# A convolution, attention and mixture-of-experts kernel: wider products, one part of each weight split moved, 24 places for gathered rows

## The reference, cut to what matters

```python
# x: (16, 16, 16, 192) float32, i.e. 4096 tokens of 192 channels
xs = gelu(x @ W1.T + b1)                 # 192 -> 48 channels
xs = abs(low_pass(xs))                   # fft2, mask, ifft2 over each 16x16 image
x  = x + (xs @ W2.T + b2)                # 48 -> 192
t  = x.reshape(16, 256, 192)
n  = layernorm(t)
q, k, v = n@Wq+bq, n@Wk+bk, n@Wv+bv      # 12 heads of 16; one k and one v head
t  = t + softmax_over_heads(rope(q).rope(k) / 4) @ v   # each token attends inside itself
n  = layernorm(t)
p  = softmax(n @ gate_w.T)               # 8 experts, the best 2 with weights p1/(p1+p2), p2/(p1+p2)
y  = sum over the 2 of  weight * ((silu(n @ gate_bank[e]) * (n @ up_bank[e])) @ down_bank[e])
out = t + y
```

## Time and profile before

| | |
|---|---|
| profiled execution | 475.46 us, span of the trace 473.7 us |
| convolution phase | 0 to 74 us |
| attention phase | 74 to 185.3 us |
| routing phase | 185.3 to 222 us |
| expert phase | 222 to 473.7 us |
| mean granted TensorE clock | 0.88 of 2.4 GHz |
| busy: PE, DVE, ACT, POOL | 394.8, 276.5, 222.0, 280.7 us |

### The profile page before, as it was taken

One profiled execution on the slowest core, in us unless ns is written; L12 is line 12 of the kernel. 1 busy time (PEld: TensorE's weight loads), 2 busy tenths in 40 slices (PEclk: granted clock), 3 DMA queues, 4 the chain that ended last, 5 costly groups with the idle time before them and its releaser, 6 DMA issues.

```text
span 473.7 us, 9033 instructions
## 1 busy us (share of the span) xinstructions
PE 394.8 (83%) x2236; PEld 373.5 (79%) x2237; DVE 276.5 (58%) x718; ACT 222.0 (47%) x513; POOL 280.7 (59%) x302
## 2 busy tenths in 40 slices
PE   5799954779888585176789999999999999999990
PEld 5799943668777474065689999999999999999990
DVE  1265683387667622997156666666666666666650
ACT  3434420434555441085245555555565556555550
POOL 0256561277777642001637877887878788787753
PEclk9999999976888555555689999999999999999996
DMA  7998532003333534200314444444445444444442
GB/s 213 245 230 227 145 68 63 25 1 103 104 102 116 148 99 137 24 0 12 104 21 68 75 78 68 72 79 72 72 73 79 68 72 77 70 73 74 59 44 25
DMA packets 46087, 41.27 MB, mean 87 GB/s; under 512 B 14153, under 2 KB 40108, under 8 KB 46060
## 3 DMA queue, kind: packets, MB, share of 16 engines
q0 software_dynamic: 14016, 17.21, 22.8%
q1 hardware_dynamic: 32044, 23.75, 18.9%
HBM read 25.87 MB, written 15.08 MB: 86 GB/s over the span
## 4 chain that ended last, share of the span: by engine, by line
PE 48%; DMA 2%; issue 1%; another core or an unknown queue 1%; ACT 0%; POOLq 0%; DVE 0%; SPq 0%; ACTq 0%; DVEq 0%
PE moe_ps_y L1137 8%; PE moe_ps_h L1123 5%; PE moe_ps_gt L1112 3%; PE moe_ps_gt L1116 3%; PE moe_ps_gt L1113 3%; PE moe_ps_gt L1115 3%; PE moe_ps_gt L1114 3%; PE moe_ps_u L1112 3%; PE moe_ps_y L1139 3%; PE moe_ps_u L1113 3%; PE moe_ps_u L1114 3%; PE moe_ps_u L1115 3%; PE moe_ps_u L1116 3%; PE moe_ps_x L1104 2%; PE moe_ps_x L1103 2%; PE moe_ps_y L1136 2%
## 5 line engine op out<-in xcount | busy, mean ns | idle before, releaser
L1078 POOL DMA_INDIRECT out<-moe_y,idx_map x72 | 114.6, 1592 | 39.8 <-issue 20.2
L1070 POOL DMA_INDIRECT moe_xt<-rows,idx_map x72 | 70.5, 979 | 55.7 <-POOLq L865 34.0
L1213 ACT ACTIVATE moe_yy<-moe_ps_y,moe_xt 128x384 f32<-128x384 f32 x72 | 41.9, 583 | 71.9 <-PE moe_ps_y L1137 58.0
L1137 PE MATMUL moe_ps_y<-wd,moe_h_hi 128*128 x216 | 71.6, 356 | 0.7 <-DVE moe_h_lo L1275 0.5
L1283 DVE TENSOR_TENSOR moe_y<-moe_yy 128x192 f32<-128x192 f32 x72 | 25.8, 359 | 57.1 <-ACT moe_yy L1213 47.7
L1193 ACT ACTIVATE moe_x_hi<-moe_ps_x 128x256 fp32r<-128x256 f32 x72 | 27.7, 385 | 38.2 <-PE moe_ps_x L1104 32.1
L1275 DVE TENSOR_TENSOR moe_h_lo<-moe_ps_h,moe_h_hi 128x384 fp32r<-128x384 f32 x72 | 40.2, 559 | 5.7 <-ACT moe_h_hi L1205 3.6
L1137 PEld LDWEIGHTS moe_ps_y<-wd,moe_h_hi 128*128 128x128 f32 x216 | 41.3, 191 | 1.3 <-issue 1.3
L1269 DVE TENSOR_TENSOR moe_hid<-moe_ps_u,moe_sg 128x384 f32<-128x384 f32 x72 | 39.4, 548 | 1.2 <-issue 1.2
L1259 DVE TENSOR_TENSOR moe_x_lo<-moe_ps_x,moe_x_hi 128x128 fp32r<-128x128 f32 x72 | 21.0, 292 | 31.8 <-ACT moe_x_hi L1193 25.3
L1205 ACT ACTIVATE moe_h_hi<-moe_ps_h 128x384 fp32r<-128x384 f32 x72 | 35.5, 493 | 4.0 <-remote 2.4
(11 more groups left out here) (188 smaller groups left out, 1124.2 us busy)
## 6 DMA issues: line engine op xcount, KB each, us to landing
xs<-in_x SPq DMA_DIRECT2D x8, 384.0 KB, 5.1
conv_stage<-in_wgu SPq DMA_DIRECT2D x8, 384.0 KB, 3.8
conv_stage<-in_wgu SPq DMA_DIRECT2D x16, 192.0 KB, 4.6
rows<-attn_xr SPq DMA_DIRECT2D x8, 384.0 KB, 2.7
out<-xs SPq DMA_DIRECT2D x8, 384.0 KB, 3.4
attn_stage<-in_down SPq DMA_DIRECT2D x8, 288.0 KB, 3.4
conv_xta<-in_xT SPq DMA_DIRECT2D x8, 256.0 KB, 4.3
moe_xt<-rows,idx_map POOLq DMA_INDIRECT x72
```

What stands on the lines that cost most here:

```text
L1070: nc.gpsimd.indirect_dma_start(xt[:, slot, :], None, rows.ap(), bass.IndirectOffsetOnAxis(ap=idx_map[:, j, 0:1], axis=0)).then_inc(gathere ...
L1078: nc.gpsimd.indirect_dma_start(out, bass.IndirectOffsetOnAxis(ap=idx_map[:, j, 1:2], axis=0), y[:, j % YR, :], None, compute_op=ALU.add).t ...
L1137: ins = nc.tensor.matmul(both, hi, halves, start=(k == 0), stop=(k == 2))
L1213: nc.scalar.activation(yy[:, s].rearrange("p h c -> p (h c)"), ps_y[:, s, 0:2 * C], ACT.Copy, scale=xt[:, slot, bass.ds(GC + e, 1)]).then_ ...
```

## The change

`XR` becomes 24, `AHEAD` 22, `YR` stays 12. `xs`, the norms' constants and the attention weights now give their room back after the attention phase, and the gathered rows lie there. The expert phase stops after 71 tiles; its loops are written out for 24 tiles; TensorE starts it with 16 matmuls whose result nobody reads, then the first transposes, then 4 more, and ScalarE with one activation of one column of the function Silu.

In the convolution phase `w1a` and `w1b` are padded with zeros to 128 columns, so that lines 240 and 241 make 128 columns; SP waits for these two memsets before its first load. `out_product` takes high and low parts stacked on 128 rows (`yt_hl`), so two matmuls do the work of three; `magnitude` has three activations for two, and the low part two subtractions for one. At the end of the phase SP issues the loads of all eight experts' down weights, straight into `wd`.

In the attention phase the router's rows are turned in six pieces of 128 columns for eight, and its logits come from three matmuls of 16 columns for each pair of tiles, six for eight. ScalarE makes all eight high parts of the down weights before `copy_products(0)`; POOL makes five of the low parts before `rotate_key(0)` and one more in each of the first three steps. POOL does `weigh_value(n)` before `deviation(n-1)`, ScalarE `exponential(n)` before `norm_route(n-2)`.

```diff
-XR = 12
+XR = 24
 AHEAD = XR - 2
-YR = XR
+YR = XR // 2
+TILES_USED = 2 * TOKENS // P + EXPERTS - 1
...
-        w1a, w1b = a.sb("w1a", [P, DH]), a.sb("w1b", [CB + 1, DH])
+        w1a, w1b = a.sb("w1a", [P, P]), a.sb("w1b", [CB + 1, P])
...
+                sp.wait_ge(wide, 2)
+                sp.dma_start(w1a[:, 0:DH], w1[0:P, :]).then_inc(w1_in, 16)
...
+                for e in range(EXPERTS):
+                    sp.dma_start(wd[:, e, :, 1, :].bitcast(F32),
+                                 down[e].rearrange("(k p) c -> p k c", p=P)).then_inc(down_in, 16)
...
-                            hi, lo = yt_hi[k, s, bass.ts(h, P)], yt_lo[k, s, bass.ts(h, P)]
-                            nc.tensor.matmul(at, hi, w2_hi[k, :], start=True, stop=False)
-                            nc.tensor.matmul(at, hi, w2_lo[k, :], start=False, stop=False)
-                            last = nc.tensor.matmul(at, lo, w2_hi[k, :], start=False, stop=True)
+                            both = yt_hl[:, s, m, bass.ts(h, P)]
+                            nc.tensor.matmul(at, both, w2_hi[:], start=True, stop=False)
+                            last = nc.tensor.matmul(at, both, w2_lo[:], start=False, stop=True)
...
-                    transposes(nc, xr[:, s], eye, ps_ra, ps_rb).then_inc(rtr_done, 1)
+                    for k in range(6):
+                        ...
+                        ins = nc.tensor.transpose(bank, flat[:, bass.ts(k, P)], eye[:])
...
-                        for t in range(QT):
-                            at = ps_q[:, s, 0, ps_lg.start + t * EXPERTS:ps_lg.start + (t + 1) * EXPERTS]
-                            nc.tensor.matmul(at, ra[:, bass.ts(t, P)], ga[:], start=True, stop=False)
-                            ins = nc.tensor.matmul(at, rb[:, bass.ts(t, P)], gb[:], start=False, stop=True)
+                        for h in range(2):
+                            pair = ps_q[:, s, 0, bass.ds(ps_lg.start + 2 * h * EXPERTS, 2 * EXPERTS)]
+                            for k in range(3):
+                                ins = nc.tensor.matmul(pair, ra[:, bass.ts(3 * h + k, P)], gates[:, bass.ts(k, 2 * EXPERTS)],
+                                                       start=(k == 0), stop=(k == 2))
...
                 out_of_psum(0, 0)
+                act.wait_ge(down_in, 16 * EXPERTS)
+                for e in range(EXPERTS):
+                    split(e)
...
                     if n < QUADS:
-                        split(*turned(0, n))
+                        exponential(*turned(0, n))
                     if 0 <= n - RING < QUADS:
                         norm_route(*turned(0, n - RING))
-                    if n < QUADS:
-                        exponential(*turned(0, n))
...
+                for e in range(EXPERTS - 3):
+                    split(e)
                 rotate_key(0, 0)
-                split(0, 0)
                 for n in range(QUADS):
                     if n + 1 < QUADS:
                         rotate_key(*turned(0, n + 1))
+                    weigh_value(*turned(0, n))
                     if n:
                         deviation(*turned(0, n - 1))
-                    weigh_value(*turned(0, n))
-                    if n + 1 < QUADS:
-                        split(*turned(0, n + 1))
+                    if n < 3:
+                        split(EXPERTS - 3 + n)
...
-                for j in range(N):
+                for j in range(TILES_USED):
                     scatter(j)
-                    if j + AHEAD < N:
+                    if j + AHEAD < TILES_USED:
                         gather(j + AHEAD)
...
+                def keep_busy(n):
+                    for _ in range(n):
+                        nc.tensor.matmul(ps_g[:, 0, 0:HID], wa_hi[:, 0, 0:P], wa_hi[:, 0, 0:HID], start=True, stop=True)
+                keep_busy(16)
                 turn_x(0, 0)
+                keep_busy(4)
```

More of the change, by code:

```diff
@@ L292, in _ @@
                 nc.scalar.activation(lp_hi[:], lp[:], ACT.Copy)
-                for k in (0, DP):
-                    b = slice(k, k + DH + 1)
-                    ins = nc.scalar.activation(w2_hi[b, :], w2s[b, :], ACT.Copy)
-                ins.then_inc(const_hi_done, 1)
+                nc.scalar.activation(w2_hi[:], w2s[:], ACT.Copy).then_inc(const_hi_done, 1)
                 def gelu(i, s):
@@ L313, in magnitude @@
                     act.wait_ge(yt_lo_done, freed(q))
-                    for dst in (yt, yt_hi):
-                        ins = nc.scalar.activation(dst[:, s, :], ps_f[:, s, 0:SEQ], ACT.Abs, bias=y_bias[:, 0:1])
+                    nc.scalar.activation(yt[:, s, :], ps_f[:, s, 0:SEQ], ACT.Abs, bias=y_bias[:, 0:1])
+                    for m in range(2):
+                        b = slice(DP * m, DP * (m + 1))
+                        ins = nc.scalar.activation(yt_hl[b, s, m, :], ps_f[b, s, 0:SEQ], ACT.Abs, bias=y_bias[b, 0:1])
                     ins.then_inc(abs_done, 1)
@@ L410, in yt_low @@
                     dve.wait_ge(w2_done, freed(q))
-                    nc.vector.tensor_tensor(yt_lo[:, s], yt[:, s], yt_hi[:, s].bitcast(F32),
-                                            ALU.subtract).then_inc(yt_lo_done, 1)
+                    for m in range(2):
+                        b, o = slice(DP * m, DP * (m + 1)), slice(DP * (1 - m), DP * (2 - m))
+                        ins = nc.vector.tensor_tensor(yt_hl[o, s, m, :], yt[b, s], yt_hl[b, s, m, :].bitcast(F32),
+                                                      ALU.subtract)
+                    ins.then_inc(yt_lo_done, 1)
                 def split(i, s):
@@ L500, in transposes, with attention_phase @@
     return ins
-def attention_phase(nc, xs, shift, rstd, eye, wqa, wqb, cos_t, sin_t, ga, gb, rows, row_tiles, down, wd, lg, out):
+def attention_phase(nc, xs, shift, rstd, eye, wqa, wqb, cos_t, sin_t, gates, rows, row_tiles, wd, down_in, lg, out):
     with ExitStack() as stack:
@@ L533, in attention_phase @@
         stored, filled, bias_row = a.sem("stored"), a.sem("filled"), a.sem("bias_row")
-        stage_in = [a.sem(f"stage_in{s}") for s in range(RING)]
         xn_done, tr_done, ev_done = a.sem("xn_done"), a.sem("tr_done"), a.sem("ev_done")
@@ L573, in store @@
                     sp.dma_start(out_tiles[:, bass.ts(q, QT), :], xs[:, bass.ts(q, QT), :]).then_inc(base_out[s], 16)
-                load_weights(0, 0)
-                load_weights(0, 1)
-                with sp.Fori(1, QUADS // RING) as i:
+                with sp.Fori(0, QUADS // RING) as i:
                     for s in range(RING):
-                        load_weights(i, s)
-                        store(i - 1, s)
-                for s in range(RING):
-                    store(last, s)
+                        store(i, s)
                 sp.wait_ge(stored, 16)
@@ L1149, in up_product, with steps @@
                     product(r, e, ps_u, HID, up_done)
-                def steps(i, first, last):
+                def steps(i, first, last, more=True):
                     e = {first: expert(i, first)}
@@ L1155, in steps @@
                         gate_product(i, r, e[r])
-                        if r + 1 < XR or last > XR:
+                        if more or r + 1 < last:
                             turn_x(i, r + 1)
@@ L1214, in weigh @@
                                          scale=xt[:, slot, bass.ds(GC + e, 1)]).then_inc(weighed, 1)
+                nc.scalar.activation(sg[:, 0, 0:1], eye[:, 0:1], ACT.Silu)
                 x_high(0, 0)
@@ L1233, in _ @@
                 n = N // XR - 1
-                for r in range(2, XR + 2):
-                    if r + 1 < XR:
+                for r in range(2, REST + 2):
+                    if r + 1 < REST:
                         x_high(n, r + 1)
-                    if r - 1 < XR:
+                    if r - 1 < REST:
                         h_high(n, r - 1)
-                    if r < XR:
+                    if r < REST:
                         silu(n, r)
@@ L1327, in _ @@
                 sp.wait_ge(meet_done, 1)
-                for j in range(1, N):
+                for j in range(1, TILES_USED):
                     if j > 1:
@@ L1332, in _ @@
                     sp.sem_inc(clear, 1)
-                for j in range(N - SR, N):
+                for j in range(TILES_USED - SR, TILES_USED):
                     landed(j)
```

115 lines of the change are left out of this document (58 added, 57 removed).

## The result

The changed kernel takes **481.56 us** (median of 4 runs, 479.83 to 483.24), the kernel before, beside it, 475.18 (470.65 to 477.8): ratio 1.014, interval 1.009 to 1.019. It is slower by 1.4%, clear of noise, and far above the 458.0 that was forecast. The profiled execution took 483.24 us with a span of 481.4, where before it was 473.7.

The account below looks back on a forecast made before the run. No single engine bounds all phases: TensorE the convolution, a three-engine ring attention, TensorE and POOL the experts. From 475.5 us, convolution -5.0, attention -9.4, routing 0 and experts -3.1 give 458.0; own range 452 to 464, of all 448 to 468.

Parts of the forecast that it names:

- What bounds the kernel, convolution: Convolution loop: TensorE bound at 7.05 us a quad, loads close behind at 6.4; the change gains 5.0 us.
- The start: Convolution: SP waits for two memsets before its first load, and loads bound the start; costs 0.8 us.
- `deviation` moves behind the weighting. The ring loses the deviation: Attention loop, POOL: the move takes the deviation out of the ring; periods fall from 10.5 to 9.1 us, 7.0 gained.
- the ring of the residual: Attention: product copy, key rotation, deviation, value weighting, residual, next copy over ScalarE, POOL and VectorE set the 10.60 us period.
- my 9.1: Attention: new period in us, taken between VectorE's 8.8 and TensorE's 9.2 with a low-clock spell.
- The first rival: Attention: TensorE at the low clock becomes the bound; half the periods so gives 466.4 us, all 475; chance 0.18.
- The collision of product and weighting: Attention: VectorE's product and POOL's weighting, side by side, take 2.29 and 1.95 us for 1.01 and 1.63.
- The tail: End of the attention phase: fewer router matmuls and transposes, less copy, 1.5 us given back by the deviation's move; 1.7 gained.
- the first scatter is at 250.4: Expert phase start: POOL issues 22 gathers at 1.25 us each, so the first scatter comes at 250.4, not 243.5.
- the second rival: Expert phase end: POOL's chain catches up at 4.8 us a scatter pair, TensorE's end counts, 8.7 gained for 3.1; chance 0.14.
- my 17.5 us: Whole kernel: the forecast gain, convolution 5.0, attention 9.4 and experts 3.1 us, from 475.5 to 458.0.
- the queue of gathers is too short: Expert phase, POOL: gathers 11 to 22 each wait for an older landing, first scatter 23 us late, 481 us; chance 0.06.

Follow-up runs that it names:

- the first four experiments: Changed kernel with 10 gathers ahead, 459.54 us; 12 places and 10 ahead, 457.01; 10 ahead then two behind each scatter, 466.14; no filling matmuls, 459.30.
- the fifth: The changed kernel run again unchanged, beside the kernel before: 461.50 us, ratio 0.979, first result 16.3 us after the first gather.

## Why the prediction was wrong

*What bounds the kernel, convolution.* Right. The in-products of quads 3 to 8 start 6.44 us apart in the mean ((50.03 - 17.84) / 5), in the 6.2 to 6.5 forecast, though single ones are 5.7 to 7.8 apart, at 239 GB/s. The clock did move, to 0.78 in the loop, up and down with each burst. The start came 0.6 us late, priced at 0.8. 4.0 us in this trace and 4.2 in the mean, for 5.0: in the tail a quad's out-products still wait 3.59 us, until 61.42, for VectorE's halves, so the faster clock gave less than 3.2.

*Attention.* Wrong in its step "`deviation` moves behind the weighting. The ring loses the deviation". The move added nothing that the traces show; the kernels with the split gone and the deviation left first are at least as short. The deviation left the ring of the residual and lengthened another that I had not drawn: copy and rotation (3.5 us), weighting (1.95), deviation (2.5), and on ScalarE the row norm (1.86), which stands ahead of the next copy in program order: with the gaps 9.9 us. I had asked what waits for POOL and forgotten that ScalarE's in-order stream carries the wait on to the copy, though the earlier trace rows and the kernel's text gave both the order and the durations. Seven periods gained 2.3 us (67.74 to 65.48) for 7.7: the last five take 50.8 us, where 9.1 each would be 45.5. The longer ring is a part of that and not the whole. With the deviation first four periods in three traces are down to 8.8 and 8.9, under my 9.1, but the five still take 50.3, 49.3 and 47.8 us. The first rival has another part: in twelve of the fourteen traces with the deviation behind, one or two of these periods are 10.5 to 11.3 us because the copy waits for TensorE, in this trace one, 11.25. What holds the other long periods no run separates. The kernel before varies too, 98.5 and 102.1 us from first copy to last router copy in its two traces. The collision of product and weighting was sized right, 2.28 us where the earlier trace rows had 2.29; the rule of the Trainium skill (SBUF — State Buffer, section "Who interferes with whom"), one after the other, would have made it 2.64, and the measurement decides against it here: both are over 2.36 us after the first began. The tail gained 3.1 us for 1.7. The deviation's move gave back 1.1 there (27.7 for 26.7), not 1.5, so the rest was worth 4.1 for 3.2.

*Routing.* Right: 37.67 us for 37.68.

*Experts.* The step that failed is the start: "the first scatter is at 250.4", 27.7 us after the first gather, priced from POOL's issue alone. It came after 38.5 us, because TensorE's signals stayed away. On the chips without the hole it is right to the tenth: 27.6 to 27.8 us in the four traces of 22 gathers unspaced. What failed there is the assumption that a longer opening row costs POOL's issue and nothing else. The trace of before held the sign, and I passed over it: ScalarE released 2.4 us late, at 236.84, by a signal that no instruction explained. I took this for start-up work; it ended with the opening row, and the change more than doubles the row.
The end was mis-sized the other way. Without the hole the pairs of scatters take 5.0 us ((445.25 - 397.65) / 19 scatters, twice), not 5.5:

```profile
397.65 1.59 POOL L1081 DMA_INDIRECT out<-moe_y,idx_map  x1 [0.30 <-issue]
...
445.25 1.55 POOL L1081 DMA_INDIRECT out<-moe_y,idx_map  x1 [0.39 <-DVE moe_y L1294]
```

So POOL, 12.5 us behind at scatter 49, has caught up at 68, and TensorE's end counts: the second rival, in its place, with 5.0 us for its 4.8 a pair. From first gather to last scatter this is 237.7 us, 7.2 less than in the trace of before, for the rival's 8.7. But that trace is from a measurement with the hole. The kernel before is 4.6 us faster where there is none (475.1 to some 470.5 us in the medians), so if the hole is all that differs, the phase gained about 2.6 us like with like, an estimate from these medians. Without the hole the change is worth 2.1%; my 17.5 us were 3.7%.

*The end.* A term was missing. After the last scatter 24 places take 7.2 to 7.8 us, 12 places 5.9 to 6.0, in every trace; it is POOL's closing step. That is 1.7 us.

*Rivals.* The third, "the queue of gathers is too short", gave 481 us, and 481.56 was measured, yet it is not what happened: gathers left every 1.25 us and landed within 3, and nothing waited for them. That the two numbers agree is luck. The right place (the opening row) with the wrong victim is not a right mechanism. The first, TensorE at the low clock, came true in part, as said.

## What to carry to other kernels

When a step is moved back on one engine, follow it through the in-order streams of the engines that wait for it, up to the first instruction of the next period: the wait is paid by what stands behind it, and the profile will call that no wait at all. A deeper prefetch is not free because its queue has room; 22 gathers ahead bought nothing over 10 or 6 in any run, cost 1.7 us at the end with their places, and 15 us more to the first result on the chip where TensorE's signals waited for the row. Before a mechanism is built on one measurement, run the same kernel once more on another chip: the first four experiments here could say nothing of the hole, and only the fifth showed it.

## What the runs showed of the hardware that was not expected

- In two of six measurements, while indirect gathers left POOL back to back at the head of a phase, TensorE's semaphores rose up to 17 us after the recorded end of its matmuls (227.54 to 244.60), while VectorE started 0.04 us after ScalarE's write (239.39, 239.43) and TensorE 0.2 us after VectorE's (240.05, 240.22); the others, on three chips, ran the same code without it.
- TensorE's granted clock in the convolution changes within a quad once the 48-column products are gone (0.78 over the loop). In the seventeen traces with wide products the first copy comes between 79.8 and 84.8 us; the level of the first attention products makes 1.3 us of that (5.4 to 6.8 us from the first of them to the copy), the rest is not explained.
- A pair of scatters with nothing between them takes 5.0 us, in the mean of 19 scatters, less than the 5.3 of the pair read from the trace of before.
- POOL's closing step grows with the places for gathered rows: 5.9 us with 12, 7.2 with 24 and 10 ahead, 7.7 with 24 and 22 ahead, 7.8 with ten gathers and then pairs.
